# Cross-attention and table-lookup FFN on one core: scratch of the FFN's indices laid out by chunk, replicated by one transfer a chunk

## What is computed

```python
x = x + xattn(layernorm(x), ctx)              # 16 heads of 32, queries and keys normalised per head,
                                              # 512 context tokens, the last 16 with keys and values of their own
h = layernorm(x)
w = lambda idx: lut[idx]                      # lut has 16 entries, idx is int32
gate, up = h @ w(gate_idx).T, h @ w(up_idx).T # both (1376, 512)
x = x + (silu(gate) * up) @ w(down_idx).T     # (512, 1376)
```

## Time and profile before

| | us |
|---|---|
| median of 3 runs | 803.06 (802.41 to 804.09) |
| the profiled execution's own time | 803.88 |
| its span | 802.1 |
| TensorE busy | 752.2 (94%) |
| VectorE busy | 518.6 (65%) |
| ScalarE busy | 495.2 (62%) |
| GpSimd busy | 265.2 (33%) |
| q1, the queue that all of SyncE's transfers go through | 28.3% of 16 engines' span, 60.29 MB |

### The profile page before, as it was taken

The page is one execution under the profiler, slowest core; times in us unless marked ns, Lnnn a source line. Parts: engine busy times, 40 slices in busy tenths (PEclk is TensorE's granted clock), DMA queues, the critical chain, the costliest instruction groups (busy, mean ns, idle before and its releaser), DMA issues.

```text
span 802.1 us, 14961 instructions
## 1 busy us (share of the span) xinstructions
PE 752.2 (94%) x5881; PEld 307.8 (38%) x5881; DVE 518.6 (65%) x1007; ACT 495.2 (62%) x1009; POOL 265.2 (33%) x276
## 2 busy tenths in 40 slices
PE   2887786999999999999999999999999999999998
PEld 1342232333443333224543332235433333265445
DVE  7979999899877994224879963228599810153221
ACT  3579889788556895662658866645489856511100
POOL 6883221000854322113843321035622310013320
PEclk9999999899999999999999999999999999999999
DMA  7649998596330000321400003222000000000001
GB/s 256 174 126 275 258 258 220 143 190 167 122 79 10 1 2 28 79 53 59 117 12 1 1 14 77 56 66 54 3 1 1 1 27 28 34 20 1 1 13 40
DMA packets 75461, 61.49 MB, mean 77 GB/s; under 512 B 34496, under 2 KB 61888, under 8 KB 75136
## 3 DMA queue, kind: packets, MB, share of 16 engines
q1 hardware_dynamic: 75056, 60.29, 28.3%
q10 hardware_dynamic: 208, 0.26, 0.1%
q0 software_dynamic: 128, 0.00, 0.0%
HBM read 43.55 MB, written 10.55 MB: 67 GB/s over the span
## 4 chain that ended last, share of the span: by engine, by line
PE 73%; DVE 16%; ACT 4%; issue 4%; POOL 3%; DVEq 0%; POOLq 0%; ACTq 0%
PE ps L1753 46%; PE ps L2120 8%; PE ps L2101 6%; PE ps L1819 5%; PE ps L2072 5%; DVE arena L1179 4%; DVE nmax L1548 3%; POOL hrstd L727 2%; ACT ps L1059 2%; PE ps L2107 2%; PE ps L1968 1%; DVE stat L1232 1%; DVE arena L1312 1%; DVE arena L1269 1%; DVE hvar L1302 1%
## 5 line engine op out<-in xcount | busy, mean ns | idle before, releaser
L1753 PE MATMUL ps<-arena,wf_hi 128*128 128x512 f16 (+1 forms) x704 | 201.4, 370 | 0.4 <-DVE arena L1192 0.4
L1059 ACT ACTIVATE ps<-ps,nmax 128x496 f32<-128x496 f32 x256 | 166.2, 652 | 23.1 <-DVE nmax L1553 23.1
L1091 ACT ACTIVATE arena<-ps 128x1024 f32<-128x1024 f32 x128 | 124.3, 1026 | 72.1 <-PE ps L2107 72.1
L1753 PE MATMUL ps<-arena,wf_lo 128*128 128x512 f16 (+1 forms) x352 | 130.0, 369 | 0.0
L1753 PE MATMUL ps<-wf_hi,arena 128*128 128x512 f16 (+3 forms) x374 | 114.8, 368 | 0.6 <-DVE arena L1196 0.6
L727 POOL TENSOR_TENSOR hrstd<-hvar,mhalf 128x16 f32<-128x16 f32 (+1 forms) x33 | 100.1, 3047 | 39.6 <-DVE hvar L1302 39.4
L1753 PEld LDWEIGHTS ps<-arena,wf_hi 128*128 128x128 f16 x704 | 64.7, 98 | 83.5 <-issue 20.5
L1179 DVE TENSOR_SCALAR arena<-arena,wf_lo 128x2048 f16<-128x2048 f16 (+1 forms) x132 | 89.6, 740 | 5.2 <-PE ps L1819 5.0
L1819 PE MATMUL ps<-arena,wf_lo 128*32 128x512 f16 (+1 forms) x1056 | 64.9, 389 | 13.0 <-ACT arena L886 9.6
L671 POOL TENSOR_TENSOR xrstd<-xvar,mhalf 128x1 f32<-128x1 f32 x32 | 24.0, 751 | 158.0 <-DVE xvar L1237 158.0
L1753 PE MATMUL ps<-wf_lo,arena 128*128 128x512 f16 (+3 forms) x187 | 68.5, 366 | 0.0
(11 more groups left out here) (164 smaller groups left out, 1051.6 us busy)
## 6 DMA issues: line engine op xcount, KB each, us to landing
arena<-idx SPq DMA_DIRECT2D x124, 128.0 KB, 3.5
arena<-in_x SPq DMA_DIRECT2D x32, 256.0 KB, 2.9
wf_lo<-in_idx SPq DMA_DIRECT2D x10, 512.0 KB, 5.1
idx<-wf_hi SPq DMA_DIRECT2D x10, 384.0 KB, 4.1
out<-arena SPq DMA_DIRECT2D x15, 256.0 KB, 2.0
wf_lo<-in_idx SPq DMA_DIRECT2D x11, 256.0 KB, 6.6
arena<-in_ctxT SPq DMA_DIRECT2D x5, 512.0 KB, 3.7
v_next<-arena SPq DMA_DIRECT2D x8, 256.0 KB, 4.2
```

The source lines that it names most:

```text
L1059: last = act.activation(sc, sc, ACT.Exp, bias=nmax[:, 0, t, h:h + 1], accum_out=den[:, 0, t, h:h + 1])
L1091: act.activation(probs[n_ % 2][:, 2 * p:2 * p + 2, :], ps[:, bank:bank + 2, :], ACT.Exp).then_inc(s["probs_set"], 1)
L1753: last = pe.matmul(dst, l, r, start=(first and i == 0), stop=(stop and i == len(todo) - 1))
```

## The change

The scratch `idx16` becomes one flat tensor in which each chunk has its own stretch of 128 x width elements, ordered k, g, n: for each k the four rows k, 32 + k, 64 + k, 96 + k stand one behind the other. A block is stored by three `dma_start`, one a chunk, with the access pattern `g k n` on the HBM side, counts 4, 32, 512, and 128 partitions by 512 on the SBUF side. A chunk is read back by one `dma_start` whose source has a leading dimension of 4 with step 0 in front of 32 rows of 2048 elements, and whose destination is 128 partitions by 2048. The counts that are waited for on `idx_out` and `rep_in` follow.

```diff
-        idx16 = nc.dram_tensor("idx16", (P, WCOLS), F16, kind="Internal").ap()
+        idx16 = nc.dram_tensor("idx16", (P * WCOLS,), F16, kind="Internal").ap()
...
             def store_idx(it):
-                cols = slice(block_at(it), block_at(it + 1))
                 sp.wait_ge(s["idx_16"], it + 1)
-                sp.dma_start(idx16[:, cols], wf_hi[:, cols]).then_inc(s[f"idx_out{it}"], 16)
+                for lo, hi in CHUNKS[3 * it:3 * it + 3]:
+                    by_group = idx16[P * lo:P * hi].rearrange("(k g n) -> g k n", k=32, g=NR4)
+                    sp.dma_start(by_group, wf_hi[:, lo:hi]).then_inc(s[f"idx_out{it}"], 16)
                 if it + STAGES < IT:
                     load_idx(it + STAGES)
 
             def load_rep(c):
                 lo, hi = CHUNKS[c]
                 if c % 3 == 0:
-                    sp.wait_ge(s[f"idx_out{c // 3}"], 16)
+                    sp.wait_ge(s[f"idx_out{c // 3}"], 16 * 3)
                 if c >= REPS:
                     sp.wait_ge(s["oh_set"], NJ * (c - REPS + 1))
                 elif c == REPS - 1:
                     sp.wait_ge(s["cT_lo"], 1)
-                src = idx16[:, lo:hi].rearrange("(g k) n -> k g n", g=NR4)
-                for r in range(NR4):
-                    dst = l_rep[c % REPS][r * 32:(r + 1) * 32, 0:NR4 * (hi - lo)].rearrange("p (g n) -> p g n", g=NR4)
-                    sp.dma_start(dst, src).then_inc(s[f"rep_in{c % REPS}"], 16)
+                n = NR4 * (hi - lo)
+                src = idx16[P * lo:P * hi].rearrange("(k n) -> k n", k=32).unsqueeze(0).to_broadcast([NR4, 32, n])
+                sp.dma_start(l_rep[c % REPS][:, 0:n], src).then_inc(s[f"rep_in{c % REPS}"], 16)
...
-                dve.wait_ge(s[f"rep_in{c % REPS}"], 16 * NR4 * (c // REPS + 1))
+                dve.wait_ge(s[f"rep_in{c % REPS}"], 16 * (c // REPS + 1))
```

## The result

| | before | after |
|---|---|---|
| median | 803.58 us (4 runs) | 897.41 us (4 runs, 896.05 to 900.74) |
| span of the profiled execution | 802.1 us | 896.8 us |
| its own time | 803.88 us | 898.64 us |
| TensorE busy | 752.2 us (94%) | 781.6 us (87%) |
| q1, share of 16 engines' span | 28.3% | 27.9% |

The ratio is 1.1174, 95% interval 1.1136 to 1.1212. The forecast was 902 us, with a range of 858 to 960.

The account below looks back on a forecast made before the run. VectorE, then TensorE, was taken to bound the kernel, with transfers hidden. Four engines' 251 us of work from 59 us end at 310, making lookup 30 98.8 us late: 902 us, range 858 to 960.

Parts of the forecast that it names:

- What bounds the kernel, and that the transfers were hidden: Turning indices into weights: VectorE sets the pace to about 140 us, TensorE from 142 to 202; replicated chunks never come late.
- SyncE's queue time: SyncE's issues: 99 fewer reads save 43 us, 22 more stores cost 9.5; the net 33 us are worth nothing.
- the sum: From 59 us, four engines carry 156 us of reads, 57 of stores, 38 of other transfers: 251, ending at 310.
- The one choice, four engines: New reads and stores: an outer count of 4 leaves 4 DMA engines working and 12 idle; 80% for both.
- A read at 5.2 us: Each chunk's read: 131,072 bytes an engine at 25 KB/us, 5.2 us, bounds 4.75 and 7.4; thirty make 156 us.
- A store at 1.9 us: Each chunk's store: 32,768 bytes an engine at 17.7 KB/us, 1.9 us, bounds 1.5 and 2.4; thirty make 57 us.
- rival 2: Only the reads are narrow, stores cost 0.5 us each: 209 us of work, delay 57, total 860 us; chance 8%.
- Lookups 31 and 32 add at most a microsecond: End of TensorE's lookups: the last two reads land 5.2 to 6.6 and 11.8 us behind, adding at most a microsecond.
- The total: Whole execution: lookup 30 comes 98.8 us late, later stages follow unchanged, so 802.1 becomes 900.9 in span; forecast 902 us.
- A delayed index load on GpSimd, 0 to 5 us: GpSimd's conversions: index loads come later behind the four engines' backlog, priced at 0 to 5 us inside the range.
- The test that I named for the profile: New profile: comparisons wait 80 to 120 us for DMA, share near 0.3, 100 GB/s, chunks 9.5 then 5.2 to 6 us.

Follow-up runs that it names:

- The pair of 804.6 and 877.6 us: Changed kernel with stores wide and one 512 KB read from the index input, not the scratch: outermost count 128 took 804.6 us, count 4 took 877.6 us.

## Why the prediction was right, step by step

- *What bounds the kernel, and that the transfers were hidden.* Right. Once the reads are spread over all engines again, in either layout, the time is back within 0.3%, so SyncE's queue time was worth nothing. But the change did not save 33 us of it: the issues of these stores and reads took 65 us before and take 115 us after, since a store of 128 KB holds SyncE 2.5 us (median) and not the 0.43 of the sum. That error costs the forecast nothing, as it counted this time as worth nothing.
- *The one choice, four engines.* Right, and this was the step on which all hung. No row of before could show it. The pair of 804.6 and 877.6 us shows that it is the outermost count and not the copies, the size or the layout of the scratch, and the packets in flight (2, 4, 8 and up to 16) show the engines themselves. The rule of the Trainium skill that was cited for it ("DMA: Bandwidth & Descriptors", "Rules for kernel authors") agrees with these runs: for counts of 2 and 4 with a step of 0, and for 4 and 8 without one. Which engines of the sixteen they are, no trace here shows.
- *A read at 5.2 us.* Measured 5.02, which is 26.1 KB/us an engine (26.5 by the mean of 106 GB/s), a little above the 25 that I took from the slices of the earlier trace rows, and above the 17.7 to 21.9 of the window means. The same page of the Trainium skill gives 435 GB/s for 16 ports ("Where 436 GB/s comes from"). Taken for one port, as an estimate, that is 27.2; the runs with two and four engines come to 96 or 97% of it.
- *A store at 1.9 us.* Too dear. I took the rate from stretches in which 16 engines pull rows of 1 KB. On four engines nearly every packet of a store, 1 KB, took 46 ns, and 32 of them make 1.5 us, my lower bound. Making the stores wide saved 23.0 us over 30 stores, 0.77 each, where the sum has 1.9 - 0.5 = 1.4. That is 19 us too much in the forecast.
- *Reads alone at 860 us (rival 2).* 14 us too little; measured 874. About half of it had come by chunk 30, which was 63.4 us late there and 56.8 in the sum, and the other half comes behind it (next point). Two sizes before chunk 30 were too small. I let two transposes and a load of x between two reads cost 1.4 + 0.7 us; the step over them is 8.6 us at chunk 26 and 7.9 at chunk 29, 3.6 and 2.9 more than a read's 5.02. And in the early part the kernel with narrow reads alone needed about 15.3 us for two chunks, where the sum has 10.4 + 1.5 + 2.8 = 14.7.
- *Lookups 31 and 32 add at most a microsecond.* Wrong: they add 7 us. The sum lets the read of chunk 32 land 11.8 us behind that of chunk 30; its comparison starts 18.65 us behind. Of these, 13.6 us are the step from chunk 31 to 32, 8.6 more than a read's 5.02. The last two transposes are a part of it. The other part is what SyncE issues behind this read while it is still under way (kernel after, SyncE):

```profile
286.51 0.78 SPq L445 DMA_DIRECT2D arena<-idx  x1
293.30 1.77 SPq L530 DMA_DIRECT2D arena<-in_x  x4
295.16 0.38 SPq L483 DMA_DIRECT2D arena<-v_next  x1
```

  These are 2 MB of loads, with no wait for this read. From 295 to 303 us a packet of 4 KB took 0.2 to 0.5 us in place of 0.159. The sum has no term for two transfers that share the four engines at the end; how much each part makes was not tried.
- *The total.* Lookup 30 was forecast 98.8 us late and was 86.4; the span was forecast 98.8 longer and was 94.7. So stores that were too dear and an end that was too cheap cancel in part, and the forecast total is better than its parts. That closeness is luck. One term of the sum, 1.5 us from the issue of the first store to its data, no row of before shows: packets of that store began 0.8 us after its issue before and 1.4 us after it in the changed kernel.
- *A delayed index load on GpSimd, 0 to 5 us.* No loss by it was found while the reads are the bound. With only the stores narrow it is what the 15 us go through, so the mechanism was seen and its price holds only beside slow reads.
- *The test that I named for the profile.* The landing was as said: 9.4 us for the first narrow read and 14 to 18 in the queue on the chain. So was the pace: 8.9 us a chunk early (said 9.5) and 5.0 with longer steps between, 6.0 on average, later (said 5.2 to 6). I wrote that the share would fall to near 0.3. It was 0.37 to 0.56 up to 200 us and about 1 from 220 us on. The rate was near 100 GB/s, as said, only from about 200 us on, and 131 to 155 before. In the same way the shares of 0.97 to 1.08 that I read as a load of all engines before are no such measure: 1.08 went with 276 GB/s and 0.96 with 187. I also put the wait for DMA at 80 to 120 us. It is 73.3, and the other 20.4 us show up as waits for TensorE; 12.1 of them stand behind ScalarE's wait for a store of values.

## What to carry to other kernels

Look at the outermost count of both sides of a `dma_start` before you look at its bytes. In these runs a leading count of 2, 4 or 8, of copies or of groups, left two, four or eight engines at work, and merging four transfers into one left a quarter of them. Whether that matters is read from bytes and not from the share: a read of 512 KB needs 5.0 us on four engines, and the stages here take 4.9 and 3.7 us a chunk, so four had no chance, with the index loads on top. A narrow transfer can also cost through its neighbours, as the narrow stores do through the index loads. A large new wait in the profile is not yet a cause. ScalarE's 15.8 us could be removed without any gain, and SyncE's stands of 11 us moved elsewhere without a loss or a gain that matters, because one set of engines set the pace.

## What the runs showed of the hardware that I had not expected

- Rows of 4 KB run at 26 KB/us an engine with two or four engines at work (53 and 106 GB/s). With eight they run so at times (159 ns a packet at 141 to 144 us) and at 15.6 when the reads follow each other (125 GB/s at 176 to 184 us), hardly more in all than four. Why is open.
- SyncE can be held in the issue of a transfer while narrow transfers are under way: up to 5.5 us for one store of 128 KB, where a store of 384 KB took 0.43 us (median) before.
- The share of the DMA engines counts waiting: 161% with four packets of the reads in flight and 106 GB/s.
